# Other order of the last three groups on each engine, smaller last segment blocks, and VectorE normalising the last group, in a two-layer graph kernel

## The reference: what is computed

```python
def layer0(V, E, src, dst):          # 8 heads of 16 features
    Q = V[src] @ Wq + bq
    K = V[dst] @ Wk + bk;  Vv = V[dst] @ Wv + bv
    scores = sum(Q * K over a head) / 4 + (E @ Wb + bb)
    alpha = softmax of scores over the edges of one dst
    return segment_sum(alpha * Vv, dst) @ Wo + bo
def layer1(x, src, dst):
    h = x @ W
    e = leaky_relu((h @ a1)[src] + (h @ a2)[dst], 0.2)
    return segment_sum(softmax(e over all edges) * h[src], dst)
x = layernorm(x + layer0(x, ...))
x = layernorm(x + layer1(x, ...))
```

## Time and profile before

| what | value |
|---|---|
| median of 3 runs | 1060.18 us |
| profiled execution, its own time | 1060.65 us |
| its span | 1058.9 us |
| busy: PE, DVE, ACT, POOL | 666.1, 806.4, 707.4, 762.0 us |
| mean granted clock of PE | 0.834 of full |
| last gather of the first stage | starts at 500.12 us |
| first gather of the second stage | starts at 531.20 us |

### The profile page before, as it was taken

How to read it: one execution, slowest core, us unless ns; L and a number is a source line. 1 busy time by engine, 2 the same in 40 slices (tenths; PEclk the granted TensorE clock), 3 DMA queues, 4 the chain that set the end, 5 groups by cost and what they waited for, 6 DMA issues and landing times.

```text
span 1058.9 us, 14567 instructions
## 1 busy us (share of the span) xinstructions
PE 666.1 (63%) x3268; PEld 451.7 (43%) x3268; DVE 806.4 (76%) x3719; ACT 707.4 (67%) x2041; POOL 762.0 (72%) x801
## 2 busy tenths in 40 slices
PE   0468777777777776788555656666566655555540
PEld 0246555555565555566445645555532111111110
DVE  4799999999998797896776767665648777777760
ACT  3669998999899797996524444444446666666660
POOL 6777777777777777777077777777737777777775
PEclk9989998999899898987858788787757778867775
DMA  7576786787777668656348888877743332332210
GB/s 196 167 230 193 223 275 213 238 264 233 221 216 243 207 219 265 206 178 220 115 131 286 269 264 255 272 241 246 236 134 92 88 93 86 88 93 84 85 47 25
DMA packets 82013, 196.90 MB, mean 186 GB/s; under 512 B 19814, under 2 KB 22005, under 8 KB 81916
## 3 DMA queue, kind: packets, MB, share of 16 engines
q1 hardware_dynamic: 56774, 148.35, 43.6%
q0 software_dynamic: 25152, 47.63, 15.8%
HBM read 122.71 MB, written 77.22 MB: 189 GB/s over the span
## 4 chain that ended last, share of the span: by engine, by line
POOL 28%; DVE 18%; issue 15%; ACT 15%; PE 10%; DMA 10%; SPq 2%; DVEq 1%; POOLq 0%; ACTq 0%
POOL xs L478 16%; POOL h_res L478 11%; DMA xs<-x_all,row_tab 6%; ACT xsT L862 5%; DVE node_out L1334 4%; DVE nst L1352 4%; ACT h_res L707 3%; PE psum L550 2%; ACT yb L707 1%; DVE match L1015 1%; DVE part L1339 1%; PE psum L662 1%; DVE nmv L1360 1%; DMA x1d_in<-x_all 1%; PE psum L656 1%
## 5 line engine op out<-in xcount | busy, mean ns | idle before, releaser
L478 POOL DMA_INDIRECT xs<-x_all,row_tab x196 | 187.6, 957 | 89.6 <-issue 83.5
L482 POOL DMA_INDIRECT out_dram<-yb,at_last x196 | 195.2, 996 | 76.2 <-issue 54.2
L478 POOL DMA_INDIRECT xs<-in_x,src_tab x196 | 187.8, 958 | 61.9 <-issue 59.1
L478 POOL DMA_INDIRECT h_res<-in_x,dst_tab x196 | 187.3, 956 | 59.7 <-issue 59.7
L707 ACT ACTIVATE h_res<-node_in,shift,rstd 128x128 f32<-128x128 f32 (+1 forms) x392 | 155.8, 486 | 0.3 <-DVE shift L1141 0.3
L682 PE MATMUL psum<-node_out,ident_inv 128*128 128x512 f32 x98 | 74.1, 847 | 96.3 <-DVE node_out L1334 96.3
L840 ACT ACTIVATE xsT<-psum 128x512 f32<-128x512 f32 x48 | 28.7, 597 | 144.8 <-PE psum L662 142.8
L1334 DVE SCALAR_TENSOR_TENSOR node_out<-node_out,same_prev,xsT 128x128 f32<-128x128 f32 x196 | 68.7, 350 | 48.7 <-ACT xsT L862 36.7
L707 ACT ACTIVATE yb<-psum,shift,rstd 128x128 f32<-128x128 f32 x200 | 75.0, 455 | 29.2 <-DVE shift L1345 26.8
L546 PE MATMUL psum<-h_res 128*128 128x512 f32 x98 | 59.2, 688 | 43.9 <-ACT h_res L714 43.9
L662 PE MATMUL psum<-ident,xs 128*128 128x128 f32 x192 | 41.8, 358 | 70.8 <-DMA xs<-x_all,row_tab 70.7
(11 more groups left out here) (277 smaller groups left out, 1808.7 us busy)
## 6 DMA issues: line engine op xcount, KB each, us to landing
x1d_in<-x_all SPq DMA_DIRECT2D x98, 256.0 KB, 2.7
node_in<-in_x SPq DMA_DIRECT2D x48, 512.0 KB
x_all<-h_res SPq DMA_DIRECT2D x48, 512.0 KB
out_dram<-node_out SPq DMA_DIRECT2D x48, 512.0 KB, 3.3
x_all<-yb SPq DMA_DIRECT2D x49, 256.0 KB, 2.4
src_b<-src_t SPq DMA_DIRECT2D x49, 256.0 KB, 7.2
node_in<-x_all SPq DMA_DIRECT2D x24, 512.0 KB, 5.7
h_res<-in_edge_attr SPq DMA_DIRECT2D x7, 784.0 KB
```

Source lines behind the costliest of these rows:

```text
L478: return pool.indirect_dma_start(out=to, out_offset=None, in_=table, in_offset=bass.IndirectOffsetOnAxis(ap=idx, axis=0))
L482: return pool.indirect_dma_start(out=table, out_offset=bass.IndirectOffsetOnAxis(ap=idx, axis=0), in_=rows, in_offset=None, bounds_check=l ...
```

## The change

The lists of the three last steps (s = 46, 47 and END = 48; TAIL = 46) are written out anew on PE, ACT and DVE. On PE the sources are turned first in them, outputs and queries follow, and only then the dst tiles are turned; the values come behind the scores. On ACT the `apply_nodes` that closed step 45 closes step 46. On DVE `add_rows` and the moments come behind the sums and shares. CAPS gets one more block: (44, 48), done while the last group is in work, and (48, 49), which has a short form (`last_cap`: one product and one sum for maximum and sum together, then the sum over the blocks); the block (36, 44) is done one step later. In the fix chain the moments of the last group go behind `hvf`, the row of x and the bias are added by PE in PSUM ahead of the last product, the ACT copy `vf` is gone (DVE reads PSUM), three small DVE operations become one (`scalar_tensor_tensor`), and the last group is normalised by four DVE operations from PSUM instead of four of ACT. FIX_ROWS is the count of ACT's steps in the fix chain.

```diff
+    TAIL = END - 2
-    CAPS = ((0, 12), (12, 24), (24, 36), (36, 44), (44, GROUPS))
+    CAPS = ((0, 12), (12, 24), (24, 36), (36, 44), (44, 48), (48, GROUPS))
@@ sync
-                    sp.wait_ge(y_applied, g + 1)
+                    if g == END:
+                        sp.wait_ge(last_applied, 1)
+                    else:
+                        sp.wait_ge(y_applied, g + 1)
@@ tensor
             def outputs(g):
+                wait(pe, y_done, g)
-            for s in range(END):
+            for s in range(TAIL):
...
+            for s in range(TAIL, END):
+                turn_src(s)
+                outputs(s - 2)
+                queries_of(s)
+                turn_dst(s)
+                keys(s)
+                turn_weighted(s - 1)
+                scores(s)
+                values(s)
             turn_src(END)
             outputs(END - 2)
             queries_of(END)
+            turn_weighted(END - 1)
             turn_dst(END)
-            turn_weighted(END - 1)
+            outputs(END - 1)
             keys(END)
-            outputs(END - 1)
+            tr(bank[2][:, 0:P], xf[:, :], ident[:, :]).then_inc(fix_pe, 1)
             scores(END)
             values(END)
-            tr(bank[2][:, 0:P], xf[:, :], ident[:, :]).then_inc(fix_pe, 1)
...
+            pe.wait_ge(sum_done, GROUPS)
+            tr(bank[2][0:H, P:2 * P], slot(run_sum[:, END, :], G), ident[:, :]).then_inc(fix_pe, 1)
             turn_weighted(END)
-            tr(bank[5][0:H, 0:P], slot(run_sum[:, END, :], G), ident[:, :]).then_inc(fix_pe, 1)
...
             outputs(END)
+            mm(bank[7][:, 0:P], ones_bf[:, :], bias_parts[:, 1, :], start=True, stop=False)
+            mm(bank[7][:, 0:P], ident[:, :], xf[:, :], start=False, stop=False)
...
-            mm(bank[3][:, 0:P], ones_bf[:, :], bias_parts[:, 1, :], start=True, stop=False)
-            pe.wait_ge(fix_act, 5)
-            mm(bank[3][:, 0:P], hfT[:, :], wo[:, :], start=False, stop=True).then_inc(fix_pe, 1)
+            pe.wait_ge(fix_act, 4)
+            mm(bank[7][:, 0:P], hfT[:, :], wo[:, :], start=False, stop=True).then_inc(fix_pe, 1)
@@ scalar
-            for s in range(FIRST, END):
+            for s in range(FIRST, TAIL):
...
-                if edge(s - 3 + AHEAD):
+                if edge(s - 3 + AHEAD) and s < TAIL - 1:
                     apply_nodes(s - 3 + AHEAD)
+            for s in range(TAIL, END):
+                weights(s - 1)
+                copy_src(s)
+                deviations(s - 3)
+                out_half(s - 4 + AHEAD - 1, 1)
+                out_half(s - 4 + AHEAD, 0)
+                queries(s)
+                copy_dst(s)
+                apply_rows(s - 3)
+                copy_weighted(s - 1)
+                if s == TAIL:
+                    apply_nodes(END)
+            weights(END - 1)
             copy_src(END)
-            weights(END - 1)
             deviations(END - 3)
             queries(END)
+            copy_weighted(END - 1)
             copy_dst(END)
-            copy_weighted(END - 1)
...
-            act.wait_ge(fix_pe, 3)
-            fn(vf[:, :], bank[0][:, 0:P], ACT.Copy).then_inc(fix_act, 1)
             deviations(END - 1)
             act.wait_ge(fix_dve, 3)
             fn(fix_args[:, :, :], fix_args[:, :, :], ACT.Exp).then_inc(fix_act, 1)
             apply_rows(END - 1)
-            deviations(END)
-            apply_rows(END)
             act.wait_ge(fix_pe, 7)
             fn(hfT[:, :], bank[1][:, 0:P], ACT.Copy).then_inc(fix_act, 1)
+            deviations(END)
...
-            fn(x1f[:, :], yf[:, :], ACT.Identity, bias=frs[:, 1:2], scale=frs[:, 0:1]).then_inc(fix_act, 1)
+            fn(x1f[:, :], bank[7][:, 0:P], ACT.Identity, bias=frs[:, 1:2], scale=frs[:, 0:1]).then_inc(fix_act, 1)
@@ vector
             def shares(g):
...
+                dve.wait_ge(v_mm, g + 1)
+            def last_cap():
+                mul = cap_mul[:, 0:2 * H * G]
+                c.link(v.tensor_tensor(mul.rearrange("p (i h t) -> p i h t", i=2, h=H),
+                                       runs[:, :, END, :].rearrange("p i (h t) -> p i h t", h=H)[:, :, :, 1:G + 1],
+                                       first_last[:, END * G:GROUPS * G].unsqueeze(1).unsqueeze(1)
+                                       .to_broadcast([P, 2, H, G]), ALU.mult))
+                c.link(v.tensor_reduce(caps[:, :, :, :].rearrange("p i h b -> p (i h) b")[:, :, len(CAPS) - 1],
+                                       mul.rearrange("p (q t) -> p q t", t=G), AX, ALU.add))
+                c.link(v.tensor_reduce(cap[:, :, :].rearrange("p i h -> p (i h)"),
+                                       caps[:, :, :, :].rearrange("p i h b -> p (i h) b"), AX, ALU.add))
-                for b, (lo, hi) in enumerate(CAPS[:-1]):
-                    if s == hi:
+                for b, (lo, hi) in enumerate(CAPS[:-2]):
+                    if s == hi + (hi == CAPS[-2][0]):
                         cap_block(b)
+            for s in range(TAIL, END):
+                attr_products(s)
+                score_rows(s - 1)
+                attr_sums(s)
+                maxima(s - 1)
+                exp_args(s - 1)
+                variances(s - 3, lambda: carry_max(s))
+                sums(s - 1)
+                carry_sum(s)
+                shares(s - 1)
+                shifts(s - 3)
+                add_rows(s - 2)
+                row_moments(s - 2)
+                products(s)
             attr_products(END)
             attr_sums(END)
             reach_of(0)
-            reach_of(1)
             score_rows(END - 1)
             maxima(END - 1)
             exp_args(END - 1)
-            carry_max(END)
-            variances(END - 3)
-            add_rows(END - 2)
+            variances(END - 3, lambda: carry_max(END))
             sums(END - 1)
             carry_sum(END)
             shares(END - 1)
             shifts(END - 3)
+            add_rows(END - 2)
             row_moments(END - 2)
+            variances(END - 2)
+            cap_block(len(CAPS) - 2)
+            reach_of(1)
+            add_rows(END - 1)
             products(END)
-            variances(END - 2)
-            add_rows(END - 1)
+            row_moments(END - 1)
+            shifts(END - 2)
             score_rows(END)
             maxima(END)
             exp_args(END)
-            shifts(END - 2)
             sums(END)
             shares(END)
...
             variances(END - 1)
-            cap_block(len(CAPS) - 1)
-            shifts(END - 1)
-            dve.wait_ge(cap_done, len(CAPS))
-            c.link(v.tensor_reduce(cap[:, :, :].rearrange("p i h -> p (i h)"),
-                                   caps[:, :, :, :].rearrange("p i h b -> p (i h) b"), AX, ALU.add))
+            last_cap()
             dve.wait_ge(fix_pe, 5)
...
+            shifts(END - 1)
+            dve.wait_ge(fix_act, 3)
+            dve.wait_ge(fix_pe, 6)
+            v.tensor_tensor(fix_s[:, 1, :], fix_args[:, 1, :], cap[:, 1, :], ALU.mult)
+            c.link(v.tensor_tensor(fix_s[:, 0, :], fix_args[:, 0, :], bank[2][:, 0:H], ALU.mult))
+            c.link(v.scalar_tensor_tensor(fix_s[:, 2, :], fix_s[:, 1, :], 1e-30, fix_s[:, 0, :], ALU.max, ALU.add))
+            c.link(v.reciprocal(fix_s[:, 1, :], fix_s[:, 2, :]))
+            c.link(v.tensor_tensor(fix_s[:, 3, :], fix_s[:, 2, :], fix_s[:, 1, :], ALU.mult))
+            v.tensor_tensor(hvf[:, :].rearrange("p (h c) -> p h c", c=HD),
+                            bank[0][:, 0:P].rearrange("p (h c) -> p h c", c=HD),
+                            fix_s[:, 3, :].unsqueeze(2).to_broadcast([P, H, HD]), ALU.mult).then_inc(fix_dve, 1)
             row_moments(END)
             variances(END)
...
-            dve.wait_ge(fix_pe, 8)
-            c.link(v.tensor_tensor(yf[:, :], xf[:, :], bank[3][:, 0:P], ALU.add))
-            c.link(v.bn_stats(fst[:, :], yf[:, :]))
+            dve.wait_ge(fix_pe, 8)
+            c.link(v.bn_stats(fst[:, :], bank[7][:, 0:P]))
             v.bn_aggr(fmv[:, :], fst[:, :]).then_inc(fix_dve, 1)
+            shifts(END)
+            dve.wait_ge(shift_done, nth(END))
+            dve.wait_ge(x1d_stored[END % YB], use(END - YB, YB) * 16)
+            for t in range(G):
+                u = nth(END) % 2
+                last = v.tensor_scalar(tile(yb[:, END % YB, :], t), tile(bank[6], t), rstd[:, u, t:t + 1],
+                                       shift[:, u, t:t + 1], ALU.mult, ALU.add)
+            last.then_inc(last_applied, 1)
```

More of the change, by code:

```diff
@@ L40, in gnn_kernel @@
     XS, XD, XDT, YB, NI, NX, NO, SB, XI = 4, 8, 2, 4, 3, 3, 2, 7, 4
-    FIX_ROWS = 7
+    FIX_ROWS = 6
     EB = 7
     assert GROUPS % EB == 0
-    CAPS = ((0, 12), (12, 24), (24, 36), (36, 44), (44, GROUPS))
+    CAPS = ((0, 12), (12, 24), (24, 36), (36, 44), (44, 48), (48, GROUPS))
     FIX = GROUPS - 4
@@ L203, in gnn_kernel @@
         fix_s = sb("fix_s", [P, 4, H])
-        xf, xfT, vf, hvf, hfT = (early(D) for _ in range(5))
+        xf, xfT, hvf, hfT = (early(D) for _ in range(4))
```

(34 more changed lines are left out.)

2 lines of the change are left out of this document (1 added, 1 removed).

## The result

After the change the kernel takes 1055.43 us (median of 22 runs, 1052.68 to 1059.72); the kernel before, run beside it, takes 1059.18 (22 runs, 1056.04 to 1061.41). The ratio is 0.9973, 95% interval 0.9964 to 0.9983; on the 1060.18 us of the start that is 1057.3, with 1056.9 forecast (the two medians alone stand as 0.9965 to 1). The 22 times lie in two heaps, 14 from 1052.7 to 1056.7 and 8 from 1058.4 to 1059.7; the experiments come back to that. The profiled execution took 1056.71 us (span 1055.0, mean granted clock 0.840).

The account below looks back on a forecast made before the run. POOL's gather and scatter issues bound the second stage, so its first gather moves the end; 1.2 + 0.3 + 1.8 = 3.3 us earlier gives 1057.35, or 1056.9 as a median, range 1055.2 to 1060.4.

Parts of the forecast that it names:

- three signs of being wrong: Granted clock under 0.9 from 493 to 515, step 47 over 10 us, or new POOL waits after its first gather.
- Rival D: Second stage takes the gain back, POOL waiting for row_tab or its ring's turned tiles: 1060.2 us; chance 0.10.
- Part 1: Steps 45 to 47, up to the products of group 47: these end 1.2 us earlier, bounds 0 and 3.2.
- (a): Late cover on DVE: moving the cap block to the end of step 45 puts copy_src 1.2 us earlier.
- (b): Late cover on ACT: moving step 45's apply_nodes, 3.17 us, lets group 46's scores end 3.2 us earlier.
- Part 2: From the products of group 47 to fix_m, DVE busy nearly throughout: 0.3 us won, bounds -1.4 and +0.7.
- Part 3: Fix chain from fix_m to x1f's store: 1.8 us won, with DVE's four PSUM operations adding 0.45.
- The transfer: Group 48's 256 KB store, now closer ahead of x1f's, may delay x1f's landing: counted 0, 0.5 us left in range.
- Rival B: PE's clock falls to its lower level in steps 47 and 48: 5.5 us lost, 1062.4 us; chance 0.09.
- the sign for part 3: What would show the fix-chain gain: 6.5 us from fix_m to x1f's store.

Follow-up runs that it names:

- before again: The kernel before the change, unchanged, traced once more; profiled execution 1058.68 us.
- nodes back: Changed kernel with apply_nodes(48) back in step 45 on ACT, ahead of queries and copy_src of 46; profiled execution 1059.98 us.
- cap back: Changed kernel with the cap block of groups 36 to 43 back in step 44 on DVE; profiled execution 1055.18 us.
- x1f first: Changed kernel with three matmuls of 48 earlier, reach_of and a cap block moved to step 46, x1f stored before group 48's rows; 1056.02 us, ratio 0.9967.
- ACT last: Changed kernel with the last group normalised by four ACT operations from PSUM instead of DVE's; 1289.79 us, one run on the slower chip.

## Why the prediction was right, and where its steps were not

The total was right, 1057.3 against 1056.9, and so was the mechanism of the largest term, the fix chain. That the two lie only 0.4 us apart is in part luck: the stretch between the stages fell by 2.64 us in the pair of profiles, and by 1.74 against *before again*, where the sum had 3.3. None of the three signs of being wrong showed in the profile of the change (clock 1.00 and 0.98, step 47 8.75 us, no new waits of POOL).

**What bounds.** POOL's first gather of the second stage moves the end, by the same amount: confirmed, 2.64 us between the stages and 2.65 of POOL's wait. It came at 527.48, with 527.9 forecast, but 1.08 us of that are the earlier last gather; counted from there it is 28.44 where the sum gives 27.8. Rival D is out.

**Part 1: 1.2 forecast, 1.36 in the pair of profiles** (2.41 to 1.05), 0.50 against *before again*. Queries of 46 went ahead of dst (483.71 and 486.60), products of 47 ended at 500.09, ACT was in `apply_nodes` when the weights of 46 were due (491.85 to 494.93), and the step from products 46 to products 47 gave back 1.86 (8.75 against 6.89; forecast 2.0). The gain stands behind the landing of dst of 46, as the forward working had it: only turn, copy and keys come between it and the products. These are the rows, before and after:

```profile
494.89 0.75 DVE L1042 SCALAR_TENSOR_TENSOR h_res<-psum,bcol,h_res 128x512 f32<-128x512 f32 x1 [0.70 <-ACT h_res L750]
```

```profile
486.60 1.11 PE L541 MATMUL psum<-ident,h_res 128*128 128x128 f32 x4 [1.76 <-DMA h_res<-in_x,dst_tab]
```

From the start of that turn (487.84 before) to the end of the products of 46 it is 7.80 us before and 4.74 after; *before again* has 8.10, nodes back 4.74, cap back 3.34, x1f first 4.29. That the two late covers named paid as well, no trace shows. With (a) taken back the products of 45 end 0.3 us nearer to the last gather, where 1.2 was forecast, and two traces of the kernel before differ by 2.3 us there. With (b) taken back PE turns dst of 46 13.7 us ahead of the last gather, no later than in the three others with the new steps (12.4 to 13.6), where the turn waits for the gathered rows (1.76 us in the changed kernel, 0.83 in cap back, 2.45 in x1f first). This part also carries the noise: over four traces with the new steps the products of 47 end between -1.87 and 1.23 behind the last gather, over two with the old at 1.55 and 2.41.

**Part 2: 0.3 forecast, 0.03 measured.** The waits went as forecast (0.83 and 0.55 became 0.30 and 0.32), and the two cap pieces cost 2.03 us (506.81 to 508.08, 515.72 to 516.48) against 1.83, the forecast 0.2. DVE's other work and handoffs took the rest, 0.5 us, and no single row holds it: from one start to the next, waits left out, the cap pieces take 2.07 us instead of 1.71, and the two `shares`, the two `add_rows`, `exp_args` and the scan of the maxima about 0.1 us more each.

**Part 3: 1.8 forecast, 1.40 measured** (8.42 to 7.02), and this is the mis-sized term: the price of DVE's four operations from PSUM. `fix_m` to `hvf` is 2.66, with 2.6 forecast. Behind it, line 1331 starts 1.46 us after the end of the moments' aggregate (521.41 to 522.87) and not 1.05: the four operations from PSUM hold it for 1.28 us (521.59 to 522.87), where I took 0.85 from the four moments of the earlier trace rows; ACT's 1.50 was the nearer row. The upper bound of +1.1 held. The estimate from the Trainium skill (VectorE: DVE Perf Modes, the section on the TRN2 errata), 1.03 us for the four, was also too low: the row has 1.36.

**The transfer: 0 forecast, 0.15 measured** (3.79 to 3.94), inside the 0.5 left. ACT last has 3.79 with the stores 1.11 us apart, and x1f landed in 1.5 us there and in 1.7 in the changed kernel, which points to the two transfers.

**Rival B was dismissed for a wrong reason.** I argued that the clock stayed full from 500 to 520 before, with PE busy 14.89 of 20 us. The new order is not the old one there: it has put four groups of cap, a `reach_of` and `add_rows` ahead of the products of 48, so that PE stands for 1.74 us ahead of the scores. I had looked for its waits in step 47. The fall comes in seven of the ten traces of the new section, but its price is 1.6 us and not 5.5, since the products of 47 to `fix_m` are bound by DVE (16.43 in nodes back too, with the fall; cap back has 16.93) and mostly outputs(48), ahead of the row of sums, is exposed. The old section has moments and variances of group 48 in that place; whether those would hide a slow PE no trace shows, as the clock was full there each time. Nodes back (30.29 us between the stages, 1059.98 us) is what a run with that fall looks like; that the upper heap of the 22 runs consists of such runs fits with it and with the 10 runs of x1f first, none of them above 1057.8, but wasn't shown run by run: 1.6 us are less than the 4 between the heaps, and the mean granted clock of a run doesn't tell them apart (0.824 to 0.839 in the upper, 0.820 to 0.841 in the lower). What makes the two heaps stays open.

**Sums.** Three are loose, and none moves a chance. Rival B's step at the lower clock is 6.9 us by 1.92 to 1.05, so 12.6 and not 12. The range's lower end counts the transfer's 0.5 as a loss; without it the bounds give 1054.7. And 8.42 less 1.8 is 6.6, where the sign for part 3 says 6.5.

## What to carry to other kernels

Where an engine waits for a landing, work ahead of that wait is covered, and what pays is a shorter list behind it: in the last steps everything that doesn't need the late rows belongs ahead of the turn. Filling the idle time of the bound engine ahead of a hand-off can starve the engine behind it (here 1.74 us on PE); look at what that one will be waiting for, and at what its clock does next. And when an operation moves to another engine and from SBUF to PSUM, price it by the row nearest in operation and operands, not by one that writes six numbers a row.

## What the runs showed of the hardware

Four `tensor_scalar` of 128x128 float32 from PSUM with two column operands took 1.36 us on VectorE, against 1.50 for the four ScalarE operations that did the same before: nearly no gain in the operation itself. TensorE's granted clock was at 1.2 GHz in part of the stretch ahead of the fix chain in seven of the eight traces in which it had waited 1.74 to 1.83 us ahead of one batch of matmuls, and in none of the six in which it had not did it fall before outputs(48) had ended. Why the fall comes after that wait, and not every time, was not isolated. And two chips ran one program 22% apart in time (1059.18 and 1293.69 us) with the same durations of single operations (eight matmuls 1.05 us, products 0.75).
